# A fused attention and feed-forward kernel: the residual sum moves from VectorE to GpSimd, and normalisation one unit back

## The reference, cut to what matters

```python
xn = _layernorm(x, axis=-1)
attn = softmax(masked scores) * query_mask[:, None, :, None]
out = jnp.einsum('bhqk,bkhd->bqhd', attn, Vh).reshape(B, T, U)
out = out + x                     # the residual sum; this x is xn
normalized = (out - mean) / jnp.sqrt(var + EPS)
s = gamma * normalized + beta
g = _silu(ffn(xn))
return x + s * g
```

## Time and profile before

| | us |
|---|---|
| median of three runs | 432.4 (432.21 to 433.94) |
| the profiled execution | 433.92 |
| its span, first to last instruction | 432.2 |
| TensorE busy | 371.8 (86%) |
| VectorE busy | 364.4 (84%) |
| ScalarE busy | 288.2 (67%) |
| GpSimd busy | 205.1 (47%) |

### The profile page before, as it was taken

The page is one execution under the profiler, slowest core; times in us unless marked ns, Lnnn a source line. Parts: engine busy times, 40 slices in busy tenths (PEclk is TensorE's granted clock), DMA queues, the critical chain, the costliest instruction groups (busy, mean ns, idle before and its releaser), DMA issues.

```text
span 432.2 us, 9673 instructions
## 1 busy us (share of the span) xinstructions
PE 371.8 (86%) x3499; PEld 244.1 (56%) x3499; DVE 364.4 (84%) x846; ACT 288.2 (67%) x572; POOL 205.1 (47%) x525
## 2 busy tenths in 40 slices
PE   0046998999989989999999999999999999999960
PEld 0013676877677764566666566566566566666420
DVE  5989999999795129998999999998998989989417
ACT  0103686898878851777778788678787778778750
POOL 8532274737632032212356465374473565565592
PEclk9999899999999999999999999999999999999995
DMA  7940003564544421256533422523323233240001
GB/s 210 314 116 1 0 2 103 137 142 135 157 112 132 116 72 45 69 127 146 140 110 91 130 72 73 128 59 104 97 70 109 82 99 102 71 106 28 3 0 49
DMA packets 32407, 41.71 MB, mean 97 GB/s; under 512 B 6136, under 2 KB 24936, under 8 KB 32360
## 3 DMA queue, kind: packets, MB, share of 16 engines
q1 hardware_dynamic: 32200, 41.08, 35.1%
q0 software_dynamic: 160, 0.03, 0.0%
HBM read 26.43 MB, written 11.02 MB: 87 GB/s over the span
## 4 chain that ended last, share of the span: by engine, by line
PE 46%; DVE 13%; issue 2%; ACT 1%; POOL 1%; DVEq 0%; ACTq 0%; POOLq 0%
PE banks L1261 16%; PE banks L1244 9%; DVE mx L1059 8%; PE banks L1224 8%; PE banks L1226 6%; PE banks L1246 5%; DVE stats L1104 2%; PE banks L1271 2%; DVE res L1098 1%; ACT pt L1179 1%; PE banks L1233 0%; DVE res L1085 0%; DVE res L1088 0%; DVE mixed L1089 0%; DVE aggr L1108 0%
## 5 line engine op out<-in xcount | busy, mean ns | idle before, releaser
L1059 DVE TENSOR_REDUCE mx<-banks 128x1 f32<-128x512 f32 (+3 forms) x352 | 200.1, 633 | 16.7 <-PE banks L1226 15.0
L1179 ACT ACTIVATE pt<-banks 128x512 f32<-128x512 f32 x320 | 169.3, 601 | 43.7 <-PE banks L1246 36.2
L1261 PE MATMUL banks<-pt,vg 128*18 128x512 f32 (+3 forms) x1024 | 81.4, 436 | 0.7 <-ACT pt L1179 0.7
L948 POOL TENSOR_SCALAR mneg<-mx 128x16 f32<-128x16 f32 x32 | 8.1, 253 | 108.2 <-DVE mx L1059 107.0
L1224 PE MATMUL banks<-k_own,q_own 76*128 76x384 bf16 (+2 forms) x192 | 48.4, 274 | 3.3 <-DVE mx L1059 2.7
L1224 PE MATMUL banks<-w_room 76*128 76x384 bf16 (+2 forms) x192 | 48.1, 274 | 3.3 <-DVE mx L1059 3.3
L1261 PEld LDWEIGHTS banks<-pt,vg 128*18 128x18 f32 x1024 | 23.7, 97 | 43.8 <-issue 33.4
L1244 PE MATMUL banks<-w_room 76*128 76x384 bf16 (+2 forms) x192 | 47.5, 275 | 0.9 <-ACT pt L1179 0.5
L1244 PE MATMUL banks<-q_own,k_own 76*128 76x384 bf16 (+2 forms) x192 | 47.8, 274 | 0.0
L1226 PE MATMUL banks<-k_own,q_own 124*128 124x128 bf16 x256 | 44.0, 219 | 0.0
L1226 PE MATMUL banks<-w_room 124*128 124x128 bf16 x256 | 43.8, 219 | 0.0
(11 more groups left out here) (199 smaller groups left out, 736.4 us busy)
## 6 DMA issues: line engine op xcount, KB each, us to landing
k_scratch<-parts SPq DMA_DIRECT2D x40, 128.0 KB, 2.3
k_own<-k_scratch SPq DMA_DIRECT2D x48, 96.0 KB
w_room<-k_scratch SPq DMA_DIRECT2D x48, 96.0 KB
q_scratch<-parts SPq DMA_DIRECT2D x24, 128.0 KB, 2.3
q_own<-q_scratch SPq DMA_DIRECT2D x32, 96.0 KB
w_room<-q_scratch SPq DMA_DIRECT2D x32, 96.0 KB
w_room<-in_w_dram SPq DMA_DIRECT2D x1, 2048.0 KB, 12.5
q_own<-q_scratch SPq DMA_DIRECT2D x16, 112.0 KB
```

Of the source, the lines that this page charges most:

```text
L1059: dve.tensor_reduce(mx[:, u % 2, heads[0]:heads[-1] + 1, q], banks[:, S0 + slots[0] % SLOTS, 0:w * len(heads)].rearrange("p (h k) -> p h k ...
L1179: act.activation(pt[:, T * j:T * j + T], banks[:, bank(), :], ACT.Exp, scale=SCALE).then_inc(exp_done, 1)
L1261: ins = mm(banks[32 * h:32 * h + VP, OT, P * k:T], vg[:, g, k, h, :], pt[:, KPLACE[k, h]:KPLACE[k, h] + n], start=(k == 0 and g % 2 == 0), ...
```

## The change

GpSimd gets a new function `residual`, called in unit 0 after `gate_in`: it waits for `att_ready`, multiplies `att` by the mask (broadcast along the features) into `res`, adds `xn_all`, and signals `res_ready`. `normalise` moves from unit 1 to unit 2, where it stands between `values_in` and `scaled`. On VectorE, `attended` of the second pair now waits for its own end and signals `att_ready`; piece 0 of `batch_stats` moves from (0, 9) to (1, 2) and, for batches 0 to 6, is only a wait for `res_ready`. Batch 7 keeps the four operations of VectorE.

```diff
@@ -872,6 +872,7 @@
         dve_self, act_self, pool_self = sem("dve_self2"), sem("act_self2"), sem("pool_self2")
         stats_ready, res_free, out_ready, out_stored = (sem(n) for n in (
             "stats_ready", "res_free", "out_ready", "out_stored"))
+        att_ready, res_ready = sem("att_ready"), sem("res_ready")
         tanh_ready, gate_free = sem("tanh_ready"), sem("gate_free")
         factors_ready, half_out = sem("factors_ready"), sem("half_out")
 
@@ -961,6 +962,14 @@
                                      v_all[:, b * TB:b * TB + TB, G * VW * g:G * VW * (g + 1)].rearrange(
                                          "p n (h w) -> p n h w", w=VW))
 
+                def residual(b):
+
+                    at = slice(b * TB, b * TB + TB)
+                    pool.wait_ge(att_ready, b + 1)
+                    link(tt(res[:, :, :], att[:, :, :], live_all[:, at].unsqueeze(2).broadcast_to([P, TB, C]), ALU.mult))
+                    link(tt(res[:, :, :], res[:, :, :], xn_all[:, at, :], ALU.add))
+                    pool.sem_inc(res_ready, 1)
+
                 def normalise(tok):
 
                     var, y = seed[:, 0], seed[:, 1]
@@ -1014,7 +1023,8 @@
                             values_in(b + 1, g - 1)
                         if g == 0 and not first:
                             gate_in(tok, b - 1)
-                        if g == 1 and not first:
+                            residual(b - 1)
+                        if g == 2 and not first:
                             normalise(tok)
                         if g == 2 and not first:
                             scaled()
@@ -1073,6 +1083,9 @@
                                  rec[:, :, :, u].unsqueeze(3).broadcast_to([P, TB, G, DH]), ALU.mult)
                     ins.then_inc(s_free, 1)
                     slots[0] += 1
+                    if pair == 1:
+                        dve.wait_ge(s_free, SLOTS + slots[0])
+                        dve.sem_inc(att_ready, 1)
 
                 def last_rows():
 
@@ -1091,14 +1104,17 @@
                 def batch_stats(tok, b, piece):
 
                     if piece == 0:
-                        dve.wait_ge(res_free, tok.next(res_free))
-                        dve.wait_ge(s_free, SLOTS + slots[0])
-                        for k in range(TB):
-                            at = b * TB + k
-                            ins = dve.scalar_tensor_tensor(out=res[:, k, :], in0=att[:, k, :],
-                                                           scalar=live_all[:, at:at + 1], in1=xn_all[:, at, :],
-                                                           op0=ALU.mult, op1=ALU.add)
-                        link(ins)
+                        if b < B - 1:
+                            dve.wait_ge(res_ready, tok.next(res_ready))
+                        else:
+                            dve.wait_ge(res_free, B)
+                            dve.wait_ge(s_free, SLOTS + slots[0])
+                            for k in range(TB):
+                                at = b * TB + k
+                                ins = dve.scalar_tensor_tensor(out=res[:, k, :], in0=att[:, k, :],
+                                                               scalar=live_all[:, at:at + 1], in1=xn_all[:, at, :],
+                                                               op0=ALU.mult, op1=ALU.add)
+                            link(ins)
                     if piece == 1:
                         for k in range(TB):
                             ins = dve.bn_stats(stats[:, k, :], res[:, k, :])
@@ -1123,7 +1139,7 @@
                             if c == 6 and g == 0 and not first:
                                 attended(tok, 1)
                             if not first:
-                                for piece, at in enumerate(((0, 9), (1, 3), (1, 6), (1, 9))):
+                                for piece, at in enumerate(((1, 2), (1, 3), (1, 6), (1, 9))):
                                     if (g, c) == at:
                                         batch_stats(tok, b - 1, piece)
                     if last:
```

## The result

The changed kernel takes 502.25 us, median of four runs (499.62 to 502.99), the kernel before in the same runs 432.6. The ratio is 1.1593, with a 95% interval from 1.1541 to 1.1644. The forecast was 487; 502.25 stands just above the upper end of its range (502), 69.7 us above the time before where 54.6 were forecast. The profiled execution took 499.62 us.

A forecast was written before the change was run, and what follows sets the result against it. TensorE was taken as the bound, VectorE mattering where TensorE waits for it. 433.9 + 31.4 + 12.2 + 10.5 = 488.0, less 1.5 for the median: 487 us; range 473 to 502, eight times in ten.

The forecast's parts named there:

- both stops: TensorE standing in unit 1 (31.4 us over 7 batches) and ahead of its transpose in unit 0 (12.2 us over 6).
- the rival of 497: TensorE's clock falls at both stops, six more slow stretches of 1.7 us than the forecast: 497 us, chance 0.25.
- Part 1: Residual sum leaves VectorE in unit 0: its maximum of chunk 10 starts 0.66 us earlier per batch.
- Part 2: Residual on GpSimd: VectorE waits 5.2 us after chunk 2 of unit 1; 4.48 us in 7 batches, 31.4 us.
- Part 3: Normalisation in unit 2 makes GpSimd's split late; TensorE stands 2.04 us in unit 0 of 6 batches, 12.2 us.
- Part 4: TensorE's clock falls to half rate at each of the 7 stops in unit 1, 1.5 us each: 10.5 us.
- long stop: TensorE's stop in unit 1, from about 245 to 248.9, then after one short chunk to 250.42, in 7 batches.
- the short one: TensorE's stop of 2.04 us ahead of its transpose in unit 0, in 6 batches; no clock fall taken.
- the row that the estimate took: Profile reading: TensorE idle 1.90 us ahead of 127.93, then 3.4 us at half rate, worth up to 1.7 us.
- The rival on the other side, faster: GpSimd's sum is ready before VectorE asks, so TensorE's wait of 0.83 us per batch goes: 427 us, chance 0.02.

The follow-up runs named there:

- normalisation alone: The kernel before with only normalisation moved from unit 1 to unit 2, the residual sum staying on VectorE: 452.11 us.
- the scaling back: The kernel with the late pieces, but GpSimd's scaling left in unit 2 behind normalisation as in the changed kernel: 451.35 us.
- filling both stops: The changed kernel with useless matmuls where TensorE stands, ahead of chunks 7 and 8 of unit 1 and the transpose in unit 0: 477.78 us.
- with the short one filled: The changed kernel with 8 useless matmuls ahead of the transpose in unit 0 only, the stop in unit 1 left bare: 493.27 us.
- The late pieces: Changed kernel with residual before gate, scaling in unit 3, VectorE's wait and statistics at chunk 8 of unit 1, aggregation and seed in unit 2: 430.54 us.
- small pieces spread: The kernel with the late pieces, with the seed at chunk 9 of unit 2 and the aggregation at chunk 10 of unit 1: 429.04 us.

## Why the prediction was right, and where its size was off

The direction, both stops, their places and their lengths came as forecast. The time did not come where the forecast put it: 480 to 493 us had the chance of 0.45, and 502.25 is nearest to the rival of 497, which had 0.25.

*Part 1* held: VectorE's maximum of chunk 10 waits for TensorE now, and without the sum the gain is 0.61 us a batch (0.66 in the text).

*Part 2* held closely in its terms: split and copy 1.59 us (330.94 to 332.53), two gate operations 2.69 (2.68 forecast), multiply and addition together 2.38 (2.46 forecast), VectorE idle 5.04 us (5.2 forecast) in 7 batches. One reading was off: the text gave the four maxima ahead of VectorE's wait 0.58 us each, from a row that has a chunk of three blocks in it; these are all four blocks wide and took 2.48 us together instead of 2.32. TensorE's stop came before chunk 7 and again before chunk 8, as described.

*Part 3* held: the split late behind 5.7 + 2.7 us, TensorE idle 1.96 us (2.04 forecast) ahead of the transpose, in batches 2 to 7. The run of normalisation alone and the run with the scaling back show that it is a loss of its own, and filling both stops gives 44.5 us of standstill for both (43.6 forecast).

*Part 4* is the step that was mis-sized. It gave the clock 10.5 us: 1.5 at each long stop, and in its words "I take no fall there" for the short one. Measured are 24.5 us. The long stop lost 2.2 us per stop (15.5 in 7, with the short one filled): the clock falls while TensorE stands and stays down for 6.8 us, twice the 3.4 us of the row that the estimate took. In that time TensorE ran one short chunk, waited 0.87 us more and then worked, and 3.8 to 5.8 us of the slow stretch fell on real work. The range of the text (0 to 3.4 us a stop) held that; the value taken was too low. The short stop lost 9.0 us (502.25 - 493.27), in 5 falls of 6 in the profiled execution, where the text took none. How the 24.5 us split between the stops depends on which is filled first, since the short one cost only 1.4 us beside a filled long one; their sum does not. Setting aside the row in hand, a fall after 1.90 us of idle time, because the loop is denser was wrong. That row was itself one outcome of two, though, as the gap of 1.88 us without a fall shows, so it could give a chance of a fall and not a count. On the rows in hand, the likeliest case should have been the rival "the clock falls at both stops" (497 us), with the long stop at its upper half.

The rule of the Trainium skill, "TensorE: Matmul & The Clock Gate", section "Why this matters for your kernels", against long idle gaps between bursts of matmuls, points the right way for the long stop. For the short one the traces differ from it: stops of 2.0 us brought the clock to half in 17 of 24 cases over four kernels.

The rival on the other side, faster, failed where the text put it: the sum must be ready when VectorE asks. The late pieces meet that; with their small pieces spread (429.04 us) VectorE asks 1 us after the sum is there, and the kernel is 1% faster than the one before.

## What to carry to other kernels

Work moved to an idle engine costs nothing only if it stands early enough in that engine's own order for who waits for it: count everything ahead of it in the queue from the moment its input is there, and place the wait for it later than that count ends. A step moved into another stage must also fit into that stage with all that already stands there; 5.7 + 2.7 us beside 1.6 of split and copy, in a stage of 7.2 us, delayed a transpose that no line of the change names. Price a stop of TensorE with its clock: here 44.5 us of standstill brought 24.5 us more of loss at the half clock, and matmuls of no use in the gaps gave those 24.5 back.

## What the runs showed of the hardware that was not expected

The slow stretches came in few lengths: 3.4 us behind stops of 1.9 to 2.0 us, and 6.8 us (once 10.2) at stops of 4.1 us followed by one of 0.9. The same stop of 2.0 us dropped the clock in 6 of 6, 5 of 6, 4 of 6 or 2 of 6 cases in kernels that differ elsewhere, and behind the same gap of 1.9 us in the first block the clock fell in some traces and not in others; why is open. Filler matmuls of 512 columns, 21 and 8 to a stop, kept the clock at 1.00 to the end of the loop. Their own cost is small, though no run shows it apart: 477.78 us, against 476.8 for the two forecast standstills added to the time before (433.2 + 43.6).
